# A three-part transformer block in fp32: the feed forward's hidden layer also made by channel, its norm folded into the output weights

## What is computed

```
x = x + xattn(layernorm(x), ctx[:, :64])     # 16 heads of 64, causal
x = x + rwkv(layernorm(x))                   # 16 heads of 8, decay, group norm, gate
x = x + ffn(layernorm(x))

def ffn(x):
    h = gelu(x @ ternary(W_fc).T)            # 128 -> 512
    h = layernorm(h) * ln_w + ln_b           # over the 512
    return h @ ternary(W_proj).T             # 512 -> 128
```

## Time and profile before

| | |
|---|---|
| median of 3 runs (lowest, highest) | 466.17 us (465.69, 466.52) |
| profiled execution: its time, its span | 466.76 us, 465.0 us |
| busy: PE, DVE, ACT, POOL | 321.6, 253.6, 205.0, 114.1 us (69, 55, 44, 25%) |
| mean granted TensorE clock | 0.85 |
| the chain that ended last, by engine | PE 42%, DVE 26%, ACT 20%, issue 7%, POOL 3%, DMA 1% |
| DMA queues over the span | 7.69 MB, mean 17 GB/s |

### The profile page before, as it was taken

The page is one execution under the profiler, slowest core; times in us unless marked ns, Lnnn a source line. Parts: engine busy times, 40 slices in busy tenths (PEclk is TensorE's granted clock), DMA queues, the critical chain, the costliest instruction groups (busy, mean ns, idle before and its releaser), DMA issues.

```text
span 465.0 us, 9098 instructions
## 1 busy us (share of the span) xinstructions
PE 321.6 (69%) x3844; PEld 261.6 (56%) x3844; DVE 253.6 (55%) x526; ACT 205.0 (44%) x409; POOL 114.1 (25%) x133
## 2 busy tenths in 40 slices
PE   1775687776677778795868677696785757667554
PEld 1655667654665567574755476565664735554244
DVE  3353446628475746645664946566657473363541
ACT  2753424624374353724382455636555252332231
POOL 1155414402232213303141222312222122020000
PEclk9959799978898969986998879989998867776566
DMA  8600000000000000000000000000000000000000
GB/s 287 235 1 3 0 2 3 0 1 1 1 2 1 2 1 14 0 1 1 1 13 1 1 1 13 1 1 1 13 2 1 1 11 1 1 11 2 0 12 11
DMA packets 4072, 7.69 MB, mean 17 GB/s; under 512 B 704, under 2 KB 2368, under 8 KB 4032
## 3 DMA queue, kind: packets, MB, share of 16 engines
q1 hardware_dynamic: 3456, 5.53, 3.3%
q10 hardware_dynamic: 576, 1.59, 1.0%
HBM read 6.06 MB, written 1.05 MB: 15 GB/s over the span
## 4 chain that ended last, share of the span: by engine, by line
PE 42%; DVE 26%; ACT 20%; issue 7%; POOL 3%; DMA 1%; POOLq 0%; SPq 0%; DVEq 0%; ACTq 0%
PE bank L299 7%; PE bank L264 6%; DVE xn_tok L717 6%; DVE s_sb L756 4%; PE bank L334 4%; PE bank L402 4%; DVE yT L822 4%; ACT o_sb L555 3%; DVE sd L828 3%; ACT w_raw L570 3%; ACT q_sb L534 2%; DVE w_raw L806 2%; ACT e_sb L542 2%; PE bank L358 2%; PE bank L238 2%
## 5 line engine op out<-in xcount | busy, mean ns | idle before, releaser
L299 PE MATMUL bank<-wo_sb,o_sb 128*128 128x128 f32 x256 | 43.7, 341 | 25.1 <-ACT o_sb L555 25.1
L548 ACT ACTIVATE pT_sb<-bank 128x512 f32<-128x512 f32 x32 | 18.2, 597 | 96.3 <-PE bank L273 96.3
L299 PEld LDWEIGHTS bank<-wo_sb,o_sb 128*128 128x128 f32 x256 | 40.6, 249 | 32.5 <-ACT o_sb L555 32.5
L991 POOL TENSOR_TENSOR s_sb<-s_sb,s_max 128x1024 f32<-128x1024 f32 x16 | 30.6, 1915 | 102.4 <-DVE s_max L762 102.4
L748 DVE TENSOR_TENSOR v_sb<-bank,bv_bc 128x512 f32<-128x512 f32 x32 | 21.5, 686 | 39.5 <-PE bank L252 39.4
L982 POOL TENSOR_SCALAR ln_var<-ln_mv 128x2 f32<-128x2 f32 x32 | 6.1, 191 | 148.6 <-DVE ln_mv L712 147.7
L997 POOL TENSOR_TENSOR e_sb<-e_sb,s_rec 128x1024 f32<-128x1024 f32 x16 | 30.4, 1901 | 46.2 <-DVE s_rec L770 46.2
L264 PEld LDWEIGHTS bank<-k_sb,q_sb 64*64 64x64 f32 x1024 | 34.7, 145 | 9.1 <-issue 6.6
L264 PE MATMUL bank<-k_sb,q_sb 64*64 64x64 f32 x1024 | 37.9, 231 | 1.5 <-DVE s_sb L756 1.5
L238 PE MATMUL bank<-cT_lo,w_hi 128*128 128x256 f32 x64 | 23.4, 366 | 20.9 <-DVE w_lo L726 10.1
L534 ACT ACTIVATE k_sb<-bank,col 128x256 f32<-128x256 f32 x64 | 26.9, 479 | 24.1 <-PE bank L240 24.1
(11 more groups left out here) (109 smaller groups left out, 786.5 us busy)
## 6 DMA issues: line engine op xcount, KB each, us to landing
out_tok<-x_tok SPq DMA_DIRECT2D x8, 128.0 KB, 1.9
w_raw<-in_w_k ACTq DMA_DIRECT2D x1, 512.0 KB, 4.9
w_raw<-in_w_q ACTq DMA_DIRECT2D x1, 512.0 KB, 6.4
w_raw<-in_w_v ACTq DMA_DIRECT2D x1, 512.0 KB, 8.0
bv_bc<-in_rows SPq DMA_DIRECT2D x1, 512.0 KB, 8.5
x_tok<-in_x SPq DMA_DIRECT2D x1, 512.0 KB, 10.3
cT<-in_ctxT SPq DMA_DIRECT2D x1, 512.0 KB, 11.1
wo_sb<-in_w_o SPq DMA_DIRECT2D x1, 512.0 KB, 11.8
```

The source lines that it names most:

```text
L299: mm = engine.matmul(b[:, 0:D], o_sb[:, t % 2, c, :], wo_sb[:, c, :], start=(c == 0), stop=(c == HP - 1))
L991: engine.tensor_tensor(s_sb[:, t % 2, :, :, :], s_sb[:, t % 2, :, :, :], s_max[:, t % 2, :, :].unsqueeze(3).to_broadcast([P, HP, 2, T]), A ...
```

## The change

The hidden layer is still made by token (`fc`, `gelu` into `h_tok`), now only for the mean and variance. It is made a second time by channel: `fc_channels` multiplies with the roles of weights and tokens swapped, and `gelu_channels` writes `hT` directly. So `turn_h`, `affine_h` and `apply_h` are gone. The norm moves behind the output matmuls: the output weights are scaled by ln_w and centred over the 512 channels (`wpr_c`, once, in `output_weights`), each token's 1/sqrt(var + eps) becomes a factor in `add_ffn`, and ln_b becomes a row `ffn_bias` that POOL adds to x_tok (`add_bias`). `ffn_out(s-2)` is done in stage s, at the place of `turn_h`, and `add_ffn(s-2)` at the place of `apply_h`. The loop has one stage less. The buffers `diag` and `ternary` of the preparation now lie in `hT`.

```diff
-            def turn_h(g, half):
-                b = take(later_banks, ("h", g, half), hT_ok, 4 * g + 2 * half + 2)
...
+            def fc_channels(g, half):
+                b = take(later_banks, ("fcT", g, half), hT_ok, 2 * g + half + 1)
+                pe.wait_ge(x3_lo_ok, g + 1)
+                pe.wait_ge(tern_ok, 1)
                 for kk in range(2):
...
+                    w = slice((2 * half + kk) * P, (2 * half + kk + 1) * P)
+                    o = b[:, kk * GTOK:(kk + 1) * GTOK]
+                    engine.matmul(o, wfc_t[:, w], x3_lo[:, :], start=True, stop=False)
+                    mm = engine.matmul(o, wfc_t[:, w], x3_hi[:, :], start=False, stop=True)
+                mm.then_inc(fcT_mm, 1)
...
+            def output_weights():
+                b = take(later_banks, "wpr_mean", wpr_ok, 1)
+                pe.wait_ge(wpr_scaled, 1)
+                for k in range(NK):
+                    mm = engine.matmul(b[:, 0:D], const[:, C_ONES:C_ONES + P], wpr_c[:, k, :], start=(k == 0),
+                                       stop=(k == NK - 1))
+                mm.then_inc(wpr_mean, 1)
+                b = take(later_banks, "ffn_bias", bias_ok, 1)
...
+                for k in range(NK):
+                    mm = engine.matmul(b[:, 0:D], col[:, COL_LNB + k:COL_LNB + k + 1].to_broadcast([P, P]),
+                                       wpr_t[:, k, :], start=(k == 0), stop=(k == NK - 1))
+                mm.then_inc(bias_mm, 1)
...
             mean_abs(1)
+            output_weights()
             turn_x(1)
...
-            for s in range(NG + 3):
+            for s in range(NG + 2):
...
-                if 0 <= s - 3 < NG:
-                    ffn_out(s - 3)
...
                     fc(s - 2, 1)
+                    fc_channels(s - 2, 0)
+                    fc_channels(s - 2, 1)
                 if now:
                     output(GT * s)
...
                     variance(s - 1)
                 if ffn:
-                    turn_h(s - 2, 0)
-                    turn_h(s - 2, 1)
+                    ffn_out(s - 2)
```

On ACT, DVE and POOL:

```diff
+            def gelu_channels(g, half):
+                act.wait_ge(fcT_mm, 2 * g + half + 1)
+                act.wait_ge(ffn_mm, g)
+                act.wait_ge(decay_ok, 2)
+                engine.activation(hT[:, 2 * half:2 * half + 2, :].rearrange("p k n -> p (k n)"),
+                                  bank[at["fcT", g, half]][:, :], ACT.Gelu).then_inc(hT_ok, 1)
...
                     gelu(s - 2, 1)
+                    gelu_channels(s - 2, 0)
+                    gelu_channels(s - 2, 1)
...
-                    affine_h(s - 2, 0)
-                    affine_h(s - 2, 1)
...
             def add_ffn(g):
                 dve.wait_ge(ffn_mm, g + 1)
-                engine.tensor_tensor(flat(group_of(g)), flat(group_of(g)), bank[at["ffn", g]][:, 0:GTOK],
-                                     ALU.add).then_inc(x3_ok, 1)
+                dve.wait_ge(bias_added, g + 1)
+                dve.wait_ge(ln_ready[LN_HIDDEN], g + 1)
+                for j in range(GT):
+                    op = engine.scalar_tensor_tensor(
+                        out=x_tok[:, GT * g + j, :], in0=bank[at["ffn", g]][:, j * D:(j + 1) * D],
+                        scalar=ln_rstd[:, LN_HIDDEN, g % 2, j:j + 1], in1=x_tok[:, GT * g + j, :], op0=ALU.mult,
+                        op1=ALU.add)
+                op.then_inc(x3_ok, 1)
...
-                    apply_h(s - 2)
+                    add_ffn(s - 2)
...
+            def add_bias(g):
+                pool.wait_ge(bias_ok, 1)
+                pool.wait_ge(x3_normed, g + 1)
+                engine.tensor_tensor(group_of(g), group_of(g), ffn_bias[:, :].unsqueeze(1).to_broadcast([P, GT, D]),
+                                     ALU.add).then_inc(bias_added, 1)
...
+                    add_bias(s - 2)
                     rstd(LN_HIDDEN, s - 2)
```

More of the change, by code:

```diff
@@ L396, in ffn_out @@
             def ffn_out(g):
                 b = take(later_banks, ("ffn", g), x3_ok, g + 1)
[L398 removed]
+                pe.wait_ge(wpr_ok, 1)
                 for j in range(GT):
                     for k in range(NK):
[L401 to L402 removed]
+                        pe.wait_ge(hT_ok, 2 * g + k // 2 + 1)
+                        mm = engine.matmul(b[:, j * D:(j + 1) * D], hT[:, k, j * P:(j + 1) * P], wpr_c[:, k, :],
@@ L859, in stats_h, with output_weights @@
                 stats(LN_HIDDEN, g, tiles_of(h_tok))
-            def apply_h(g):
-                apply(LN_HIDDEN, g, tiles_of(h_tok), h_tok, h_normed)
             def add_ffn(g):
                 dve.wait_ge(ffn_mm, g + 1)
-                engine.tensor_tensor(flat(group_of(g)), flat(group_of(g)), bank[at["ffn", g]][:, 0:GTOK],
-                                     ALU.add).then_inc(x3_ok, 1)
+                dve.wait_ge(bias_added, g + 1)
[6 more added lines that the diff above has]
+                op.then_inc(x3_ok, 1)
+            def output_weights():
+                dve.wait_ge(tern_ok, 2)
+                dve.wait_ge(ld_col, 16)
+                for k in range(NK):
+                    op = engine.tensor_scalar(wpr_c[:, k, :], wpr_t[:, k, :], col[:, COL_LNW + k:COL_LNW + k + 1], None,
+                                              ALU.mult)
+                op.then_inc(wpr_scaled, 1)
+                dve.wait_ge(wpr_scaled, 1)
+                dve.wait_ge(wpr_mean, 1)
+                for k in range(NK):
+                    op = engine.scalar_tensor_tensor(out=wpr_c[:, k, :], in0=bank[at["wpr_mean"]][:, 0:D],
+                                                     scalar=-float(D), in1=wpr_c[:, k, :], op0=ALU.mult, op1=ALU.add)
+                op.then_inc(wpr_ok, 1)
+                dve.wait_ge(bias_mm, 1)
+                engine.tensor_copy(ffn_bias[:, :], bank[at["ffn_bias"]][:, 0:D]).then_inc(bias_ok, 1)
             def ternarise(i, raw, dst):
```

37 lines of the change are left out of this document (13 added, 24 removed).

## The result

| | before | after |
|---|---|---|
| median of the runs (lowest, highest) | 466.35 us (465.69, 468.25) | 516.1 us (513.0, 519.68) |
| profiled execution: its time, its span | 466.76, 465.0 us | 518.25, 516.5 us |
| mean granted TensorE clock | 0.85 | 0.805 |

The changed kernel is slower: the ratio is 1.1062 [1.0971, 1.1153]. The forecast was 515.5 us. The kernel before has one run more here than ahead of the prediction, so its median differs a little. Every ratio leaves disturbed runs out, while medians and ranges hold all runs.

A forecast was written before the change was run, and what follows sets the result against it. The prediction took a chain of hand-overs, with no engine full, to bound the kernel. Its terms summed to +49.3 on the profiled 466.76, so 516.1, and 515.5 us for the median; range 485 to 536.

The forecast's parts named there:

- part 1: Stages 2 to 6, gelu(0) to kv: fc_channels in front of output delays kv by 5.0 us each, +25.0.
- part 2: Stages 2 to 6, DVE's queue: add_ffn waits for ffn_out ahead of group_norm, 4.0 us each, +20.0.
- part 3: Head of stages 3 to 7: ffn_out and add_ffn gone, 2.2 us each, -11.0; stages 8 and 9, -3.0.
- part 4: Stage heads: PE's longer wait for zT starts rwkv_out and scores at half clock, 1.5 us five times, +7.5.
- all the rest: Removed transposes, affine activations and apply_h, gelu_channels on ACT and add_bias on POOL: taken at nothing.
- The clock guess: After about 4 us without matmuls, fc_channels starts at half clock and PE recovers within output; 5.0 us taken.
- Part 5: End of the kernel, after the second gelu: 5.3 us instead of 10.0, a gain, -4.7.
- stages 7, 8: Stages 7 and 8: fc_channels ahead of kv +3.0 and +1.7; add_ffn in DVE's queue +2.5 and +3.6.
- Part 6: Preparation: output_weights holds PE and delays ACT's decay loop, scores(0) near 42.1 instead of 37.40, +4.7.
- DVE beside POOL: normalise on POOL beside group_norm on DVE: 0 to 1.9 us a stage, taken as 0; skill's rule, 0.3 for L831.
- Neither wait hid in the other: Rival that only one new wait counts: without add_ffn's wait 482 us, 6%; without the wait ahead of kv 486, 7%.
- The clock rival: PE stays at half clock through the projections too, some 4 us more in five stages: 535 us, 9%.

The follow-up runs named there:

- The experiment: The changed kernel with fc_channels moved on PE from in front of output(2s) to right behind it: 504.41 us, ratio 1.0777.
- the kernel with both moves: The changed kernel with fc_channels moved behind output(2s) on PE and add_ffn behind stats_3 on DVE: 470.84 us, ratio 1.0053.
- switched off alone: The changed kernel with eight matmuls on constants in front of rwkv_out in stages 2 to 6, in PE's wait for zT: 510.5 us, ratio 1.0913.
- The kernel with banks of its own: The changed kernel, fc_channels behind output and in attention's banks, its second half behind rwkv_rg, add_ffn at stage's end, output_weights in stage 0: 447.88 us; repeated 447.62 us.

## Why the prediction was right, point by point

The sum can be set against the trace over stages 2 to 6 (us; the intervals are those of the chain in each stage):

```
                                          forecast  after - before
part 1: gelu's end to kv                   +25.0      +25.3
part 2: variance's end to the reciprocal   +20.0      +17.4
part 3: ffn_out and add_ffn at the head    -11.0      -10.6
part 4: rwkv_out and scores                 +7.5       +8.9
all the rest                                 0         -0.7
stages 2 to 6                              +41.5      +40.3
```

- **Part 1** (5.0 a stage). Gelu's end to kv is 4.66 instead of 0.04 in stages 3 and 4, a loss of 4.6, and 5.3 to 5.5 in the other three. The clock guess held: eight matmuls and output ran at 0.60 in the mean. The experiment confirms the mechanism (3.2 of it went with the move), and shows what the part did not say: its price is not separable from the clock elsewhere in the stage.
- **Part 2** (4.0 a stage). The reciprocal is 3.8 behind variance instead of 0.53, so 3.3 in stage 4 and 3.7 in stage 3. The term was 0.3 to 0.8 too high, 2.6 in the five stages; in stage 4 ffn_out took 1.80 us, not 2.3. Taking add_ffn out of the queue's way gave 32 to 37 us with part 4, where the two were put at 26.1 + 7.5.
- **Part 3** (-2.2 a stage). Exact in the kernel with both moves, 1.78 + 0.42, and 14 us when done alone in the kernel before, as summed, though not in the places where it was booked.
- **Part 4** (+1.5 a stage). In the heads of stages 3 to 7 scores took 1.2 to 1.6 more, rwkv_out 0.1 to 0.5 more; switched off alone it gave 5.6 to 6.9, for 7.5. The estimate was somewhat low because of the row that it took for half clock: the 1.63 for 32 matmuls was partly at full clock (0.72 in the mean from 249.8 to 256.0 of the kernel before), and the same 32 took 1.90 in after, where the window stands at 0.50.
- **Part 5 and stages 7, 8.** Together +3.1 was forecast and +4.5 came. Stage 8 is as foreseen, ffn_out at half clock 3.43 and the reciprocal at 498.45, behind it. From apply_3's start to the end of the last add_ffn it is 9.1 us, against 14.1 before: 5.1 less, where 4.7 was booked. What the sum lacked lies in stage 7: between kv and variance four groups of matmuls (L340, L354, L305, L369) took 1.5 us more in all than their like before.
- **Part 6** (+4.7). Two errors of opposite sign. The delay of scores(0) came out at 3.5, since DVE's scaling took 0.89 (not 1.1), the second eight matmuls 1.71 (not 1.9), and turn_x(1) with its copy and POOL's part 1.35 up to the decay loop (not 2.1). But stage 0 then took 3.4 us more with unchanged instructions, which no term held.
- **DVE beside POOL**, taken at nothing: L850, the product behind the reciprocal, took 0.62 in stage 4, with normalise running until 306.45, and 0.50 in stage 8, where POOL was idle. In the kernel with both moves, where normalise is over by then, its own duration is 0.48 to 0.49 in all eight stages, against a median of 0.61 in after. So 0.12 a stage, 0.6 us in all. The reciprocal itself did not stretch (1.71, and 1.76 before). The Trainium skill's rule (SBUF — State Buffer, Who interferes with whom) gave the right instruction and 0.3; the trace shows less than half of that.
- **The rivals.** Neither wait hid in the other: each experiment that removes one leaves the other's cost. The clock rival did come in, but small: 277 to 286 ran at 0.50, and the middle of stage 4 (269.6 to 283.2) had 0.73. It cost 1.9 us there, from kv to centring, and nothing in the other four stages, where I had given it 4 us in each; the dense middle of the kernel before was not at full clock either (0.55 in the earlier trace rows).

The median agrees with the forecast to 0.6 us, closer than the parts deserve. By the spans it is 51.5 against 49.3: stages 2 to 6 were put too high by 1.2 and the preparation by 1.2, while stage 0 and the last stages were put too low by 3.4 and 1.4. The mechanism of parts 1 to 4 is shown; that the errors came to so little is luck. What the forecast left at nothing, the clock of instructions that the change doesn't touch, was worth 3.4 us in stage 0, 1.9 in stage 4 and some 1.5 in stage 7.

## What to carry to other kernels

On an engine that works in order, ask of each moved step what it waits for and what is queued behind it, before asking what it costs: here one step of 0.6 us on DVE cost over 30 us by its place, and the same change with three steps moved and fc_channels in other banks is 4% faster than the kernel before. A shared PSUM ring is such a queue too: a new user of it makes the next user wait for the new user's reader. And try the place without the rest of the change: two thirds of the best version's gain (14 of 21 us) came with the move of ffn_out and its add alone.

## What was not expected of the hardware

- Stage 0 took 39.6 us in two of the profiled executions and 42.7 to 43.2 in nine others; six of the nine have the same instructions there as the first of the two, three the same as the second. Where the instructions are the same and scores(0) start 0.4 us apart or at the same time, the windows differ by their granted clock (1.00 against 0.70 and 0.79, or 0.96 and 0.79). That is over 3 us, and no difference in the program there goes with it.
- A stretch of PE without any pause (277.0 to 286.0 in after) stayed at 1.2 GHz for 9 us. The kernel with banks of its own ran the matmuls of that stretch up to L258 (248.6 to 253.3 there) at 2.4 GHz. So a removed wait of 3.2 us made stage 4 only 1.8 us shorter in one case, and in another a wait of 1.43 went and the stage was 3.5 us shorter.
- What decides which of the two a stretch gets is left open: the runs show which kernels got it, and none was made to tell its rule.
